# Graph attention walk: the place of the score maximum in VectorE's order, and three of eight pairs kept in DRAM

## The reference

```
feat = (h @ W).reshape(N, H, D)
e = leaky_relu(el[src] + er[dst], 0.2)
ex = exp(e - segment_max(e, dst)[dst])
alpha = ex / segment_sum(ex, dst)[dst]
rst = segment_sum(feat[src] * alpha[..., None], dst) + bias
```

## Time and profile before

| what | us |
|---|---|
| median of 3 runs (the lowest 6528.30) | 6529.58 |
| profiled execution, its own time | 6532.67 |
| its span | 6530.9 |
| PE busy in the span | 5098.4 (78%) |
| DVE busy | 3381.7 (52%) |
| ACT busy | 2222.7 (34%) |
| POOL busy | 2219.6 (34%) |
| gathers of the rows (L690), busy | 1738.4 |

### The profile page before, as it was taken

The page is one execution under the profiler, slowest core; times in us unless marked ns, Lnnn a source line. Parts: engine busy times, 40 slices in busy tenths (PEclk is TensorE's granted clock), DMA queues, the critical chain, the costliest instruction groups (busy, mean ns, idle before and its releaser), DMA issues. The chain is left out here.

```text
span 6530.9 us, 127122 instructions
## 1 busy us (share of the span) xinstructions
PE 5098.4 (78%) x34156; PEld 4113.7 (63%) x34157; DVE 3381.7 (52%) x10342; ACT 2222.7 (34%) x6042; POOL 2219.6 (34%) x2057
## 2 busy tenths in 40 slices
PE   2665655428888888884797899999899997299997
PEld 1443332215555555554796688887788886299997
DVE  6898766528888888887455421113411114422222
ACT  0345666615555555556232300001200002433332
POOL 2577777765555555552221000000000000612221
PEclk8898777669999999995898999999999997599998
DMA  4478888875555555554565244442222223466665
GB/s 134 129 234 273 278 287 289 290 196 146 146 147 146 146 148 146 146 147 129 163 179 163 79 162 162 152 161 100 72 98 93 94 98 118 133 187 181 181 182 165
DMA packets 504762, 1057.75 MB, mean 162 GB/s; under 512 B 59670, under 2 KB 370317, under 8 KB 484972
## 3 DMA queue, kind: packets, MB, share of 16 engines
q1 hardware_dynamic: 385276, 706.86, 34.2%
q0 software_dynamic: 112144, 268.88, 15.0%
q10 hardware_dynamic: 7200, 80.28, 3.1%
HBM read 741.74 MB, written 323.21 MB: 163 GB/s over the span
## 5 line engine op out<-in xcount | busy, mean ns | idle before, releaser
L690 POOL DMA_INDIRECT arena<-table,arena x1664 | 1738.4, 1045 | 980.3 <-DVE arena L795 584.7
L1303 PE MATMUL banks<-arena 128*128 128x256 bf16 x14700 | 1623.7, 273 | 24.7 <-DMA arena<-counts 24.7
L1303 PEld LDWEIGHTS banks<-arena 128*128 128x128 f16 x14700 | 1439.5, 98 | 205.0 <-DMA arena<-counts 25.5
L869 PE MATMUL banks<-arena 128*128 128x261 f32 x3328 | 1009.5, 428 | 192.2 <-DVE arena L807 125.1
L620 PE MATMUL banks<-arena 128*128 128x392 bf16 x2368 | 602.2, 408 | 414.2 <-ACT banks L648 226.5
L2026 POOL DMA_INDIRECT expert_in<-arena,slot x147 | 161.2, 1097 | 2158.1 <-DVEq L1971 2116.4
L869 PEld LDWEIGHTS banks<-arena 128*128 128x128 f32 x3328 | 596.7, 199 | 330.5 <-DVE arena L807 134.0
L620 PEld LDWEIGHTS banks<-arena 128*128 128x128 bf16 x2368 | 338.2, 149 | 677.7 <-issue 635.4
L1357 DVE TENSOR_TENSOR rings<-rings,banks 128x256 f32<-128x256 f32 x98 | 41.3, 422 | 1344.1 <-PE banks L1295 1344.1
L2209 ACT ACTIVATE rings<-banks,b_sb 128x128 f32<-128x128 f32 x1296 | 370.5, 369 | 828.3 <-PE banks L2242 828.3
L795 DVE TENSOR_TENSOR arena<-arena 128x512 f32<-128x512 f32 x832 | 575.3, 692 | 141.4 <-ACT arena L742 140.4
(11 more groups left out here) (344 smaller groups left out, 5444.0 us busy)
## 6 DMA issues: line engine op xcount, KB each, us to landing
arena<-counts SPq DMA_DIRECT2D x100, 1568.0 KB, 6.7
arena<-in_L_ffn_W SPq DMA_DIRECT2D x114, 1024.0 KB, 5.2
edge_rows<-arena SPq DMA_DIRECT2D x416, 264.0 KB, 3.3
arena<-edge_rows SPq DMA_DIRECT2D x416, 264.0 KB, 2.9
counts<-arena ACTq DMA_DIRECT2D x50, 1568.0 KB, 6.8
arena<-in_L_ffn_w SPq DMA_DIRECT2D x64, 1024.0 KB, 5.2
expert_in<-arena SPq DMA_DIRECT2D x25, 2028.0 KB
arena<-table,arena POOLq DMA_INDIRECT x1664, 3.9
```

What stands on the lines that cost most here:

```text
L690: pool.indirect_dma_start(out=got[:, u, j, :], out_offset=None, in_=table0, in_offset=bass.IndirectOffsetOnAxis(ap=src_sb[:, 2 * pair + j: ...
L869: last = pe.matmul(banks_a[u][:, 0:mw], onehot[:, u, j, :], msg[:, u % RB, j, 0:mw], start=(j == 0), stop=(j == 1))
L1303: last = pe.matmul(psum[u][:, 0:D], a_ring[:, u, a, :], parts[:, a, k, :], start=(a == 0 and k == 0), stop=(a == NT - 1 and k == 2))
```

## The change

Two edits. The set of kept pairs goes from (0, 2, 4, 6) to (0, 3, 6), so `LIVE` becomes (1, 2, 4, 5, 7): three pairs of eight are gathered ahead and read back, five are gathered during the walk. And in the walk's body on VectorE collect moves from behind left to the end, with the one-hot now ahead of the maximum: sum, messages, left, one-hot, maximum, collect.

```
-KEPT = (0, 2, 4, 6)
+KEPT = (0, 3, 6)
...
                                 if two:
                                     score_left(*two)
-                                collect(i, u, tile(u))
+                                if u + RB + 1 < UN or not final(i):
+                                    make_onehot(i + (u + RB + 1) // UN, (u + RB + 1) % UN)
                                 if two:
                                     score_max(*two)
-                                if u + RB + 1 < UN or not final(i):
-                                    make_onehot(i + (u + RB + 1) // UN, (u + RB + 1) % UN)
+                                collect(i, u, tile(u))
```

## The result

The changed kernel takes 6363.0 us (median of 4 runs, 6359.96 to 6366.45), against 6529.8 us before: a ratio of 0.9745, 95% interval 0.9728 to 0.9762. That is 167 us less where 215 were forecast. One of the four executions of the kernel before took 12715.31 us and is left out of the ratio; the median of the other three is 6529.58 us.

A forecast was written before the change was run, and what follows sets the result against it. POOL's issue rate bounds the stage before the walk, a ring of VectorE and ScalarE the walk. Profiled 6532.7 - 118.8 - 2 - 100 + 7 = 6318.9, less 3 for the median: 6315 us, range 6275 to 6365.

The forecast's parts named there:

- the main term: Start of the walk: the first addition of scores no longer waits 118.8 us for the read-back of edge_rows.
- the 1134 of the terms: Early gathers during the fill: 624 gathers end at 1120 us, the first step's five live pairs add 14 us.
- a tie of ScalarE's ring and collect's register work: VectorE's period in the walk: 1.56 us through ScalarE's activations against 1.57 with collect's register work exposed; 1.57 taken.
- the sum: VectorE's instruction starts added up within a walk pair: max to messages 0.67 us, collect 1.11 us after messages.
- So POOL is no bound today but comes within a few tenths of the new step: GpSimd in the walk: five pairs' gathers per step still fit the new step of 13.49 us.
- Five are 12.75 us per step, 12.9 by the walk's mean gather: GpSimd's walk load: five pairs per step at 2.55 us each, two gathers and two gaps of 0.30 us.
- the price beside the fill: GpSimd's dearest estimate: 1.35 us per gather as beside the busy fill, 13.5 us per walk step.
- Two of the signs that the prediction gave for being wrong: In the walk: left waits for gathers, and POOL is never idle.
- rival B: Walk: order gains nothing, period stays 1.70 us or POOL keeps the step near 14.5; 6410 us, chance 0.06.
- rival A: Walk: VectorE holds up gathers, GpSimd bounds, slower than before; by the skill's rule 19.4 us steps, 6929 us; chance 0.01.
- I keep their number and add 36 x 0.2 = 7 us: TensorE's lower-clock stretches in the walk: about 36 remain, each costing 1.2 us instead of about 1.
- the net of my two terms: The walk's gain from the new order: 100 us from shorter steps less 7 us for low-clock stretches, 93 us.

The follow-up runs named there:

- the order alone: Kernel before with only VectorE's order changed, four of eight pairs kept: 6411.46 us, ratio 0.9815.
- the weights in PSUM: Changed kernel, ScalarE writing the exponential first to PSUM for VectorE's messages, then to SBUF for TensorE: 6285.3 us, ratio 0.9628.
- the constants in PSUM: Changed kernel, messages multiplied by constants from a PSUM bank instead of the weights in SBUF, output not the layer's: 6286.53 us, ratio 0.9629.

## Why the prediction was right, and where it missed

The direction and the main term held. The wait of 118.8 us went in full. The last early gather began at 1150.4 us, some 17 us later than the 1134 of the terms (1120 and 14), but far ahead of the fill's end, so nothing hung on it. The fill gave 6 us where the forecast had 2 for its last store and 0 for the rest.

The step of VectorE held almost to the number. The period is the 1.57 us forecast as a tie of ScalarE's ring and collect's register work (2011.77 - 2010.20). Max starts 0.20 us after the one-hot (2011.09 - 2010.89) and 0.28 after left, the messages 0.68 after max, as in the sum. Collect starts 1.06 us after the messages (2011.26 - 2010.20), and the sum had 1.11. The 36 undisturbed steps of the changed kernel take 13.53 us, for 13.49 forecast.

The step that missed is "So POOL is no bound today but comes within a few tenths of the new step", by its term "Five are 12.75 us per step, 12.9 by the walk's mean gather". A gather beside the new walk costs 1.14 us (789.17/693) and not 0.99, with its gap 1.44, and ten are 14.4 us: the mean step. The 13.5 us at the price beside the fill, the dearest in that sum, were too few as well. Two of the signs that the prediction gave for being wrong have come, waits of left for gathers and a GpSimd that is hardly ever idle in the walk, although the time lies in the range.

The price was read from gathers that the messages barely touched. In the kernel before, the first of a pair is released by the end of the messages and takes 0.95 us. The second begins 0.50 us after the next start of the messages: in the rows on record the messages start at 2013.98, and the gather that begins at 2014.48 takes 1.00 us, so it ends 1.50 us after them. I read the 0.05 us as the whole price of running beside VectorE ("The trace disagrees so far (0.05 us, not 0.69)"). They were the tail of a hold: only 0.19 us of the messages were left when this gather began. Another pair of the same trace shows more of it:

```profile
2007.16 0.69 DVE L795 TENSOR_TENSOR arena<-arena 128x512 f32<-128x512 f32 x1 [0.20 <-ACT arena L742]
```

```profile
2007.57 1.10 POOL L690 DMA_INDIRECT arena<-table,arena  x1 [0.30 <-issue]
```

This gather begins 0.41 us after the messages and ends 1.51 after them. In the walk of the kernel before 381 gathers begin 0.15 to 0.52 us after a start of the messages, and all end 1.50 to 1.53 us after it. The hold could be read there before any run.

The size of the step stood among the rivals, in the second half of rival B, "POOL at 1.45 us per gather keeps the step near 14.5", with a chance of 0.06 for all of B. Its time of 6410 us did not follow from it: 14.43 us is a mean step, and the mean step before was 14.76, not the 14.45 of an undisturbed one. The mechanism stood in rival A by the rule of the Trainium skill (SBUF — State Buffer, section Who interferes with whom), and I set it aside. The runs agree with the rule: with a product of two SBUF inputs gathers take 1.14 us in the mean, with one input in PSUM 0.95. They also show why it did not give A's 19.4 us: a gather is only held where it begins under the messages, and then for less than is left of them, which makes it 0.3 to 0.5 us longer in the lock and not 0.69 each.

The second miss has the other sign. "I keep their number and add 36 x 0.2 = 7 us": their number was right for the kernel before (37 steps over 15 us), but with the order alone only six disturbed steps are left, the clock is 0.99, so 1% in place of 4% short of full, and that run gives 119 us, 26 more than the net of my two terms.

The traces split the gain. The walk starts 125 us earlier. From its first to its last messages it takes 1538 us before, 1417 with the order alone, 1494 in the changed kernel and 1416 with the weights in PSUM. So the order is worth 121 us, the held gathers take 77 of them back, and 125 + 121 - 77 = 169 us is the gain, against 167 between the medians and 171 between the profiled runs. With the weights in PSUM 245 us are there. Set against the forecast's own terms, 214 - 77 + 28 + 4: the miss of 77 us was covered for 28 by the order (121 for 93) and for 4 by the fill (6 for 2). Without that cover the time would have been outside the range.

## What to carry to other kernels

A duration read where an engine waits before each instruction is the price at that phase, not the price of a full queue: before work is moved to an engine, ask what its instructions will begin under once they run back to back. Read a duration together with its place: a few hundredths of a microsecond more can be the end of a long hold. Where one engine's instruction holds another engine's, the holding can lock the second to the period of the first, here nine gathers per step where ten were needed. Taking one operand of the product out of SBUF was worth an extra activation of 0.19 us per pair here: 78 us less. Measure each of two edits alone: here one of them by itself made its own stage slower (15.20 us per step for 14.76) and the sum hid it.

## What was not expected of the hardware

The end of a held gather does not depend on when it began: 1.49 to 1.53 us after the start of the messages, in both orders of VectorE. The lock of GpSimd to VectorE's period (seven gathers of 1.40 us in a row) follows from it, since 1.51 and the gap of 0.30 us less the period of 1.70 is again 0.11 us after a start of the messages.

The holding also goes the other way, but briefly. Where a gather begins 0 to 0.04 us after the messages, it takes its free 0.95 us and the product is the longer one, as here in the changed kernel:

```profile
2053.38 0.76 DVE L795 TENSOR_TENSOR arena<-arena 128x512 f32<-128x512 f32 x1
```

```profile
2053.42 0.95 POOL L690 DMA_INDIRECT arena<-table,arena  x1 [0.30 <-issue]
```

In this walk 26 of the 832 products take 0.72 to 0.76 us in place of 0.68 to 0.69; with one input in PSUM none takes over 0.69. So the two take turns, and the gather's own turn is a short one, 0.08 us at most (0.76 less 0.68).

The messages are not the only instruction that holds. With the constants in PSUM 91 gathers begin about 0.8 us after the messages, under the one-hot, whose two inputs are both in SBUF and which ends 0.97 us after the start of the messages. They take 1.00 to 1.04 us and end at 1.78 to 1.80, again 0.82 us after the end of the instruction that held them.

And the granted clock of TensorE rose from 0.96 to 0.99 in the walk by the new order of three VectorE instructions alone, which left VectorE's busy time per pair nearly as it was (1.53 and 1.54 us) but shortened its idle time between. TensorE was 81% busy at 0.96 and 85% at 0.99. What of this keeps the clock up was not tested.
